# Constant products in the waits of TensorE, and a reordered drain, in a vision-transformer block

## What is computed

```python
h = tokens(x)                                     # patches @ W + b, cls in front
h = h + attn(layernorm(h))
h = h + ffn(layernorm(h))

# attn: q, k, v by projection, causal convolution over 4 tokens, silu; q, k normed
Sn = a * (St - b * Sk[:, :, None] * kt[:, None, :]) + b * vt[:, :, None] * kt[:, None, :]
ot = einsum('bij,bj->bi', Sn, qt)                 # for every token in turn
return (rmsnorm(o) * norm_w * silu(x @ Wg.T)) @ Wo.T + bo

# ffn
gh = relu(einsum('bsd,hd->bsh', x, gfc1_w) + gfc1_b)
g = (einsum('bsh,eh->bse', gh, gfc2_w) + gfc2_b).mean(axis=1)   # one g for an image
W1m = W1 + einsum('be,efd->bfd', g, tv_W1)        # and W2m, b1m, b2m alike
lng = ln_g + 0.03 * (tv_ln_g - ln_g).sum(axis=0)  # and lnb alike
out = relu(x @ W1m.T + b1m) @ W2m.T + b2m
return layernorm(x + out) * lng + lnb
```

## Time and profile before

| | us |
|---|---|
| median of 3 runs (lowest, highest) | 891.03 (890.76, 892.22) |
| profiled execution | 895.05 |
| its span | 893.2 |
| TensorE busy in the span | 838.4 (94%) |
| VectorE, ScalarE, GpSimd busy | 664.9, 482.1, 355.4 |
| mean granted clock of TensorE | 0.975 of full |

### The profile page before, as it was taken

The page is one execution under the profiler, slowest core; times in us unless marked ns, Lnnn a source line. Parts: engine busy times, 40 slices in busy tenths (PEclk is TensorE's granted clock), DMA queues, the critical chain, the costliest instruction groups (busy, mean ns, idle before and its releaser), DMA issues. The chain is left out here.

```text
span 893.2 us, 31060 instructions
## 1 busy us (share of the span) xinstructions
PE 838.4 (94%) x11766; PEld 634.7 (71%) x11766; DVE 664.9 (74%) x2420; ACT 482.1 (54%) x1721; POOL 355.4 (40%) x530
## 2 busy tenths in 40 slices
PE   5689999999999999999999999999985999999996
PEld 2357777777777777777777777777764677777775
DVE  3466888888888888888888888888764676868434
ACT  0434455565655565565655565566523355666654
POOL 3122333233332332233332332333211178888875
PEclk9999999999999999999999999999958799999999
DMA  2000121222111110111110110111100233333431
GB/s 62 10 13 12 48 54 49 59 60 59 38 53 48 36 32 24 36 36 37 32 35 24 33 34 24 37 31 30 28 26 24 90 96 111 107 107 114 122 119 43
DMA packets 78659, 45.33 MB, mean 51 GB/s; under 512 B 20357, under 2 KB 69803, under 8 KB 78511
## 3 DMA queue, kind: packets, MB, share of 16 engines
q1 hardware_dynamic: 77663, 42.80, 16.8%
q10 hardware_dynamic: 848, 0.54, 0.2%
HBM read 23.69 MB, written 19.63 MB: 49 GB/s over the span
## 5 line engine op out<-in xcount | busy, mean ns | idle before, releaser
L1050 PE MATMUL bank<-SA,work 128*128 128x386 f32 x200 | 93.5, 550 | 6.5 <-ACT work L528 6.5
L1647 PEld LDWEIGHTS bank<-work 128*128 128x128 f32 x768 | 89.6, 192 | 12.5 <-issue 12.5
L1529 ACT ACTIVATE work<-bank,b1mix 128x512 f32<-128x512 f32 x96 | 66.0, 687 | 59.4 <-PE bank L1621 59.3
L438 ACT ACTIVATE logit<-bank 128x2 f32<-128x2 f32 x100 | 17.3, 173 | 149.3 <-PE bank L1051 149.1
L1647 PE MATMUL bank<-work 128*128 128x128 f32 x768 | 89.9, 275 | 0.8 <-DVE work L1407 0.8
L616 POOL TENSOR_SCALAR var2e<-mv 128x4 f32<-128x4 f32 x25 | 5.7, 227 | 211.1 <-DVE mv L795 211.1
L1621 PE MATMUL bank<-work 128*128 128x512 f32 x192 | 86.5, 593 | 0.0
L1051 PE MATMUL bank<-SB,work 128*128 128x256 f32 x200 | 60.8, 386 | 0.0
L1621 PEld LDWEIGHTS bank<-work 128*128 128x128 f32 x192 | 34.6, 190 | 34.6 <-issue 34.4
L1010 PEld LDWEIGHTS bank<-work 32*32 32x32 f32 x3200 | 35.6, 108 | 32.9 <-issue 27.2
L1051 PEld LDWEIGHTS bank<-SB,work 128*128 128x128 f32 x200 | 38.9, 194 | 27.9 <-issue 1.8
(11 more groups left out here) (233 smaller groups left out, 2287.8 us busy)
## 6 DMA issues: line engine op xcount, KB each, us to landing
hn_kept<-work SPq DMA_DIRECT2D x25, 256.0 KB, 2.3
hnT_kept<-work SPq DMA_DIRECT2D x25, 256.0 KB, 2.3
work<-hnT_kept SPq DMA_DIRECT2D x25, 256.0 KB, 2.9
work<-hn_kept SPq DMA_DIRECT2D x25, 256.0 KB, 3.1
out_dram<-work SPq DMA_DIRECT2D x24, 256.0 KB, 2.5
tv<-in_L_ffn_tv_W_dram SPq DMA_DIRECT2D x16, 256.0 KB
work<-r_kept SPq DMA_DIRECT2D x25, 98.0 KB
work<-in_x_dram SPq DMA_DIRECT2D x23, 102.0 KB
```

What stands on the lines that cost most here:

```text
L1050: mm(t[:, 0:386], xs[p][:, b, HIST:XW], SA[:, 0:386], start=True, stop=False)
L1529: ins = nc.scalar.activation(hid[f][:, :], ps[:, :], ACT.Relu, bias=b1mix[:, of[0], f:f + 1])
L1647: ins = mm(by4(bank[2 + par])[:, t, :], hid[f][:, t * C:(t + 1) * C], w2T[of[t]][:, f, :], start=(f == 0 and t == 0), stop=(f == FB - 1), ...
```

## The change

Four things are done, all in the drain and at the gate. `tail` is true for j = 24, 25 and 26.

1. `keep_busy(n)` issues n products of the identity with itself into bank 2, which nobody reads. They stand in iteration 24 between the halves of the levels, in 25 ahead of Z and pz, in 26 ahead of the last transposes, and twice at the gate. A wait for the last decay scan, which reads bank 2, is put ahead of iteration 24.
2. In the drain the second norm (statistics and hn on VectorE, the power on GpSimd, the transposes and the gate product on TensorE, the copy on ScalarE) stands behind the sixth level, and ahead of og and its transposes. `values` (vt) moves behind the fifth block.
3. `tensor_early` runs in iteration 26, ahead of the last transposes, and takes the first product of the mixed W2 (L1593) with it.
4. GpSimd waits for its own `knorm` ahead of the copies of Y, in all iterations.

The steps that move became functions; their text is the same. Moved bodies are left out here.

```diff
 # scalar
-                if on(j, LH):
-                    ...hnT
+                if on(j, LH) and not tail:
+                    gate_tokens()
                 ...Y5, X5, cdecay, X6
+                if on(j, LH) and tail:
+                    gate_tokens()
                 ...ogT, relu
 # gpsimd
                     pool.wait_ge(Y_ready, 5 * (s + 1))
+                    pool.wait_ge(knorm_ready, s + 1)
                 ...copies of Y and X, oscale, knorm
+                if on(j, LH) and tail:
+                    norm2_factor()
 # vector
                 grow(1)
+                if on(j, LH) and not tail:
+                    norm2_statistics()
                 ...
                 new_blocks(3)
+                if on(j, LH) and not tail:
+                    norm2()
                 ...
                 new_blocks(4)
+                if on(j, LI) and not tail:
+                    values()
                 grow(4)
                 ...o
                 new_blocks(5)
+                if on(j, LI) and tail:
+                    values()
                 ...decay, ovar, kn2, xs, state, qn2e
                 new_blocks(6)
+                if on(j, LH) and tail:
+                    norm2_statistics()
+                    norm2()
                 ...og
 # tensor
+                def keep_busy(n):
+                    for _ in range(n):
+                        mm(bank[2][:, 0:D], ident[:, :], ident[:, :], start=True, stop=True)
+                tail = j >= STEPS - 1
+                if j == STEPS - 1:
+                    pe.wait_ge(decay_ready, STEPS)
                 ...km
                 if H_:
+                    if tail:
+                        keep_busy(3)
                     ...wo
                 level_blocks(1)
+                if tail and I_:
+                    keep_busy(2)
                 level_update(1)
+                if tail and I_:
+                    keep_busy(4)
                 if C_:
+                    if j == STEPS:
+                        keep_busy(7)
                     ...Z
                 level_blocks(2)
+                if tail and I_:
+                    keep_busy(2)
                 level_update(2)
                 ...qm
                 level_blocks(3)
+                if tail and I_:
+                    keep_busy(2)
                 level_update(3)
+                if tail and I_:
+                    keep_busy(4)
                 level_blocks(4)
                 if C_:
+                    if j == STEPS:
+                        keep_busy(5)
                     ...pz
                 level_update(4)
                 ...dm
                 level_blocks(5)
+                if tail and I_:
+                    keep_busy(2)
+                if H_ and not tail:
+                    gate_tokens()
                 level_update(5)
+                if tail and I_:
+                    keep_busy(5)
                 level_blocks(6)
+                if tail and I_:
+                    keep_busy(3)
+                if H_ and not tail:
+                    gate_hidden()
                 level_update(6)
+                if H_ and tail:
+                    if j == last:
+                        ffn["tensor_early"](pe)
+                        keep_busy(14)
+                    gate_tokens()
+                    keep_busy(4)
+                    gate_hidden()
                 ...transposes of og
 # second part, tensor_early and tensor
         ins.then_inc(ln_ps, 1)
+        nc.tensor.matmul(bank[3][:, 0:HALF * D], ident[:, :], w2nat[:, 0:HALF, :].rearrange("p a c -> p (a c)"), start=True, stop=False)
-        tensor_early(pe)
+        keep_busy(8)
         pe.wait_ge(gh_ready, 1)
         ...L1589, L1590
-        mm(half2, ident[:, :], w2nat[:, 0:HALF, :].rearrange("p a c -> p (a c)"), start=True, stop=False)
+        keep_busy(3)
         pe.wait_ge(g_ready, 1)
```

More of the change, by code:

```diff
@@ L441, in kvg_out, with gate_tokens @@
                         nc.scalar.activation(kvg[s % 3][:, b, :], bank[4 - b % 2][:, 0:384], ACT.Silu).then_inc(kvg_ready, 1)
+                def gate_tokens():
+                    s = j + LH
+                    act.wait_ge(hnT_ps, s + 1)
+                    need(act, gf_ps, s)
+                    need(act, hnT_out, 16 * s)
+                    nc.scalar.copy(hnT, by4(bank[6])).then_inc(hnT_ready, 1)
+                tail = j >= STEPS - 1
                 kvg_out(0)
@@ L599, in body, with norm2_factor @@
                 p = 1 - par
+                def norm2_factor():
+                    s = j + LH
+                    pool.wait_ge(mv2_ready, s + 1)
+                    need(pool, rstd2_ready, s)
+                    apart(pool)
+                    nc.gpsimd.tensor_scalar(var2e[:, :], mv2[:, :, 1], EPS, None, ALU.add).then_inc(var2e_ready, 1)
+                    pool.wait_ge(var2e_ready, s + 1)
+                    need(pool, hn_ready, s)
+                    nc.gpsimd.tensor_tensor(rstd2[:, :], var2e[:, :], half_neg[:, :], ALU.pow).then_inc(rstd2_ready, 1)
+                tail = j >= STEPS - 1
                 if on(j, LE):
@@ L654, in body @@
                     nc.gpsimd.tensor_tensor(knorm[:, :], kn2[:, :], half_pos[:, :], ALU.pow).then_inc(knorm_ready, 1)
-                if isinstance(j, int) and j == first:
+                if on(j, LH) and tail:
+                    norm2_factor()
+                if j == first:
                     level_masks()
@@ L1051, in kvg_rows, with gate_tokens, gate_hidden @@
                     mm(t[:, 0:256], xs[p][:, b, 1:1 + C], SB[:, 0:256], start=False, stop=True).then_inc(kvg_ps, 1)
+                def keep_busy(n):
+                    for _ in range(n):
+                        mm(bank[2][:, 0:D], ident[:, :], ident[:, :], start=True, stop=True)
+                def gate_tokens():
+                    pe.wait_ge(hn_ready, h + 1)
+                    if C_:
+                        pe.wait_ge(o_ready, c + 1)
+                    for b in range(NB):
+                        ins = tr(by4(bank[6])[:, b, :], hn[:, b, :], ident[:, :])
+                    ins.then_inc(hnT_ps, 1)
+                def gate_hidden():
+                    pe.wait_ge(hnT_ready, h + 1)
+                    if I_:
+                        pe.wait_ge(Y5_ready, s0 + 1)
+                    mm(bank[1][:, :], gfc1_T[:, :], hnT.rearrange("p b c -> p (b c)"), start=True, stop=True).then_inc(gf_ps, 1)
+                tail = j >= STEPS - 1
+                if j == STEPS - 1:
+                    pe.wait_ge(decay_ready, STEPS)
                 if C_:
```

55 lines of the change are left out of this document (40 added, 15 removed).

## The result

| | before | after |
|---|---|---|
| median (lowest, highest), 4 runs each, us | 891.62 (890.76, 892.81) | 902.44 (901.91, 905.17) |
| ratio to before, 95% interval | | 1.0118 [1.0099, 1.0137] |
| profiled execution, its span, us | 895.05, 893.2 | 902.34, 900.6 |
| mean granted clock of TensorE | 0.975 | 0.991 |

The change makes the kernel 1.2% slower, 10.8 us by the medians, although TensorE's clock is higher. The sign and the cost of the new order were as predicted, and so was the sum against the profiled execution (902.05 forecast, 902.34 found), this last in part by errors that cancel. The median was not: 902.44 against 898.0, inside the stated range (892.5 to 903.0), but above the 894 to 902 of the forecast itself.

What follows compares the result with a forecast made beforehand. Took the drain (648 to 715 us) as holding the whole effect, with two half-clock pieces, then VectorE's merging. Order -0.8 + 5.3 - 2.4 = +2.1, cold 2.0 + 1.6 + 1.3: +7.0 on 891.03, 898.0 us (892.5 to 903.0).

Steps and rivals of the forecast that it cites:

- levels of j=24: Six inverse levels in the drain: 6.6 us won, half by the held clock, half by norm 2 moving out.
- rest of j=24: Level 6's end to the next wo: late norm leaves 0.8 of 6.6 us won; cold adds 1.6 us.
- j=25, order and cold: Norm ahead of og in iteration 25: +5.3 us by order, +2.0 us by cold behind the 6 to 7 us hole.
- j=26: Iteration 26 and gate products at full clock: transposes 0.5, gate product 1.0, second gate product 0.95 shorter; -2.4 us.
- gate to first add: After the gates, a 4 us idle stretch may leave weight-mixing products at half clock: +1.3 us, from 0 to 3.4.
- what comes ahead of j=24: Everything before the drain: nothing of the change reaches it, 0 us.
- carrying over the 4.0 us: Whole kernel: the median lies 4.0 us below the profiled execution after the change too, giving 891.03 + 7.0 = 898.0.
- TensorE runs at full clock from the start to 648 us: Before the drain: read from the page's clock line, whose digits below 9 are only the 30th to 32nd.
- (1): Drain and gate: clock holds in all holes, only order counts, +2.1 us, 893.1 us (892 to 894); chance 0.12.
- (2): og in j=24 and 25: late oscale hides norm 2; 884.5 us, or 889 if in one iteration; chance 0.06.
- (3): Levels of j=24: fill doesn't hold the clock and products overrun; 903 us (900 to 908); chance 0.08.
- (4): Drain: gains and losses cancel, levels 2.2 us each, cold stretches shorter than priced; 890 to 892 us; chance 0.04.

Runs made afterwards that it cites:

- holes_filled: Kernel after, with 14 more constant products ahead of the moved transposes in j=24 and 28 more in j=25: 899.38 us, ratio 1.007.
- before_again: Kernel before, run again with no edit: 893.68 us, ratio 0.9999; its profiled execution took 891.36 us.
- fill_only: Kernel after, with second norm and vt in their old places in j=24 and 25, without the four products behind the moved transposes: 890.13 us, ratio 0.9969.
- fill_light: `fill_only` with fewer constant products in j=24: none ahead of wo, 1, 2, 2 and 1 between levels instead of 2, 4, 5 and 3: 888.25 us, 0.9947.
- norm24_old: Kernel after, with the second norm back in its old place in j=24 alone, without the four products behind its moved transposes: 896.13 us, ratio 1.0043.
- fill_2526: `fill_only` with no constant products in j=24, those in j=25, j=26 and at the gate kept: 890.34 us, ratio 0.9982.
- norm25_old: Kernel after, with the second norm back in its old place in j=25 alone, without the four products behind its moved transposes: 895.49 us, ratio 1.0026.
- after_again: Kernel after, run again with no edit beside the kernel before: 903.46 us, ratio 1.012.

## Why the prediction was right or wrong

**The sum against the profiled execution.** Differences of the two rows of the table, and what the steps had said:

| us | predicted | first profiles |
|---|---|---|
| levels of j=24 | -6.6 | -5.2 |
| rest of j=24 (level 6's end to wo25), order and cold | +7.4 | +7.3 |
| j=25, order and cold | +5.3 and +2.0 | +6.8 |
| j=26 | -2.4 | -2.4 |
| gate to first add | +1.3 | 0.0 |
| what comes ahead of j=24 | 0 | +0.9 |
| sum | +7.0 | +7.4 |

The agreement of the sums is luck in part: the levels won 1.4 us less than forecast and 0.9 came ahead of j=24, while the gate's 1.3 did not come and j=25 cost 0.5 less. The signs came in their order, each some 2 us late: level 6's end at 666.16 (near 664 forecast), the cold of j=25 from about 686 (684), wo of j=26 at 694.91 (690 to 693).

**j=25, right.** The order costs 5.4 us by `holes_filled`, 5.3 predicted, by the mechanism named: og waits behind the norm on VectorE, and its transposes behind the gate product on TensorE. The cold behind the hole cost 1.4 in the first profile instead of 2.0.

**j=24 behind the levels, right.** Level 6's end to hn is 3.25 us (3.3 predicted), hn to wo 5.76 (4.2 and 1.6 of cold), and 4.35 with the clock held. The three products ahead of wo cost 0.67 us (km to wo 1.56 us, against 0.89 in `before_again`), 0.7 predicted. The Trainium skill (TensorE: Matmul & The Clock Gate, Part 2, Step-by-step: what each phase is for) has matmuls in program order; this 0.67 us and the 1.4 us between the levels of `fill_only` and `fill_light` agree with it.

**The levels, near in sum against that profile (5.2 us won, 6.6 forecast), wrong in their reasons.** I had split the 6.6 us half to the clock, half to the norm's moving out. By `norm24_old` the norm's part is 1.15 us. By the two profiles of the kernel before the clock's part is 5.8 us (24.42 against 18.59). And the fill takes 1.7 us back (20.32 against 18.59), of which 1.4 go with the lighter fill; the sum priced only 0.7, for the three products ahead of wo. 24.42 - 5.8 + 1.7 - 1.15 = 19.2, which is what the levels took.

**The gate, wrong.** TensorE's longest idle piece there is 1.96 us and not 4, and the clock held. The price was wrong too: in `fill_only`, `fill_2526`, `norm25_old`, `holes_filled` and the second profile of the kernel after the clock did fall at the gate, and the segment took 17.23 to 17.40 us, against 17.31 and 17.32 in the three profiles where it held. VectorE's merging, whose last step for the first group ends 15.1 us behind the gates (721.97), ends later than TensorE's cold products and hides them. That GpSimd's adds would stretch as many merging steps as before, three, was right.

**The step that failed: carrying over the 4.0 us.** I took the 4.0 us by which the profiled execution of the kernel before lay above its median for something that every profiled execution has. Were it so, the median after would be about 898.3, the 902.34 of the profile less 4.0. But in all later kernels the profiled execution is itself one of the runs, and it lies on either side of their median: at it in the kernel after (902.34 and 902.44), 2.2 us above it in `after_again`, 2.3 below it in `before_again`. The two profiles of the kernel before differ by 3.7 us: the second is 5.8 shorter in the levels, by the clock that it kept there, 1.5 longer in j=25, where it lost the clock, and 0.8 later at the start of j=24. How much of the scatter of the other runs comes from the levels is not shown, for they have no trace. But each lists its mean granted clock. There are 77 runs of the kernel before, beside the experiments and in `before_again`, with a correlation of time and clock of -0.74; the four values with most runs:

| mean clock | runs | median us | lowest, highest |
|---|---|---|---|
| 0.975 | 13 | 895.22 | 894.83, 895.78 |
| 0.978 | 23 | 892.86 | 892.06, 893.95 |
| 0.982 | 14 | 891.36 | 890.27, 894.55 |
| 0.983 | 9 | 890.92 | 890.39, 893.39 |

The profile that I walked (895.05 us, clock 0.975) is at the slow end of these, and the three runs whose median I added to (891.03) are at the fast end. Against a profile with the levels warm, the change wins nothing in them and pays the holes in full: 66.26 to 77.18 us in the table, +10.9, close to the difference of the medians. The sum against that profile is: levels +0.6 (the fill's 1.7 less the norm's 1.15), rest of j=24 +7.7 (9.0 against 1.33), j=25 +5.3 (against the 14.49 of this profile, which had a cold piece there), j=26 -2.4, gate -0.2: +11. So the term that was mis-sized for a median is the levels' -6.6. That this profile (891.36) stands for the four runs before (median 891.62) is read from their times alone, for those runs have no trace.

It also follows that "TensorE runs at full clock from the start to 648 us" was wrong. The page's digit is 9 from 90% up, and a cold piece of a few us hides in a slice of 22.3. Two stretches of the kernel before:

```profile
46.00:48.00 2.00, 1.53 (x34) 1.19 (x35) 1.25 (x4) 0.00 (x0) 0.00 (x0) 0.64 0.15 45
48.00:50.00 2.00, 2.00 (x36) 1.01 (x34) 0.00 (x0) 0.45 (x2) 0.00 (x0) 0.50 0.06 15
```

In `before_again` this piece is longer (44 to 52 us), and `fill_only` and `fill_light` have a further one at 62 to 70. These pieces shift what follows: from a row of TensorE ahead of them (L1155 of the kernel before, at 41.36 us in its first profile) to the first wo it is 52.25 us in that profile, 53.57 in `before_again` and 55.87 in `fill_only`. The +0.9 us ahead of j=24 are of another kind, for 0.76 of them are there at that row already (42.12 us in the kernel after). The change to GpSimd's wait, the only piece of the edit that acts before the drain, stays in the other edited kernels, and some of these start j=24 as early as 646.1, as the kernel before does; so it is scatter of the start, and what sets it is open.

**The rivals.** That the clock holds in the holes (1) did not happen; when it was made to hold, +5.4 and +4.5 us of order were left, so the late norm loses with a full clock too. That og hides the norm (2) fails in both iterations: oscale ends 4.5 us ahead of og in j=24 and 3.9 in j=25. That the fill does not hold the clock in the levels (3) is wrong in every profile with fill in j=24. 903 came out nearly as it said, for another reason. The cancelling (4) would have needed levels of 2.2 us each; from wo's end (649.60) to level 6's end (666.16) they took 16.6 us, 2.8 each.

## What to carry to other kernels

Before a step is moved behind a stage to clear that stage, ask what waits behind it at the new place: the second norm cost nothing in a hole of VectorE, and 5.4 us ahead of og with the clock held. Constant products are cheap where TensorE waits anyway and are paid in full, 0.22 us each, where it does not; try fewer, as long as the trace shows that the clock holds. And before a profile is walked, compare its mean clock and time with those of the other runs of the kernel: a sum made against an execution at the slow end must not be added to a median from the fast end.

## What the runs showed of the hardware

One kernel can keep or lose TensorE's clock in the same instructions: the same six levels, with km and wo ahead of them, took 24.42 us in one execution and 18.59 in another, and over 77 runs, from 890.3 us to 897.5, the time went with the mean clock (correlation -0.74). The Trainium skill (TensorE: Matmul & The Clock Gate, Part 1, What's actually happening) says that the number of cold matmuls at the start of one kernel varies from run to run, and puts the penalty of this warm-up under 1% of a typical span. The traces agree that the cold varies; the scatter here, 0.8%, holds cold pieces in the middle of the kernel as well as early ones. It is two thirds of what the change cost.

What a cold piece costs depends on what sets the end there: at the gate, where VectorE's merging ends last, the clock at 0.50 left the segment at 17.36 us (17.31 with the clock held), while behind the holes of j=24 and j=25, where TensorE's products stand in the chain, it cost 1.4 us each in the first profile of the kernel after, and 2.9 in j=24 of `norm25_old`.
